# Cross-attention of a decoder layer: the softmax sums of four heads in one group of matmuls

## The chip, the cores and the metric

The kernel runs on one core of a Trainium2 chip. The metric is the time of one execution on the device, in microseconds (us). The engines are PE (matrix multiplication), DVE (vector), ACT (scalar functions), POOL (GpSimd) and SP (here it only issues DMAs). Each works through its own queue of instructions in order; they wait for each other by semaphores.

## What is computed

One decoder layer over 4 x 512 tokens of width 512, in fp32: self-attention (32 heads of 16, causal), cross-attention, and a feed-forward part with quantised weights and activations, each on the layer norm of its input and added to it. The change lies in the cross-attention:

```
qh = q.reshape(b * h, d // h, m)          # b = 4, h = 8: 32 heads of 64 rows
kh = k.reshape(b * h, d // h, -1)         # k and v are both the context
vh = v.reshape(b * h, c // h, -1)
qk = einsum('bdm,bdn->bmn', qh, kh) / sqrt(d // h)
sm = softmax(qk, axis=-1)                 # over 512 columns n
ret = einsum('bmn,bcn->bcm', sm, vh)      # 64 rows x 512 per head
x = x + ret
```

## The kernel before

`rest_of_layer` (line 891) holds three parts: the output projection of self-attention (`attend_output`), the cross-attention (`attend_context`) and the feed-forward part (`feed`). `in_turn` (line 972) gives each engine the same order of steps, so the order in which an engine meets its work is written out by hand: attention steps i = 3 to 43, and from step 36 on a feed body beside each (body 2 beside step 36, and so on); then the rest of the feed bodies, up to body 19.

The 32 heads go in 16 pairs p. Head j of a pair uses half of the partitions. The stages of one pair lie several steps apart; `pair_due(i, behind)` says which pair is due in step i, and gives one in every second step only. In a step i the engines meet:

- PE: two rounds of F (`first_scores`, line 1592: two matmuls, for head i - 1, each into one of three PSUM banks) and S (`second_scores`, line 1612: eight matmuls for head i - 4, with a row of maxima subtracted; banks from a pool of four). Then, in even steps, the sum of pair (i - 8) / 2 (`sum_probs`, line 1651) and half of W (`weigh`, line 1637: probabilities times context) of pair (i - 6) / 2; in odd steps the other half of W, of pair (i - 5) / 2.
- DVE: four reductions (line 1416), each of which frees a bank of F. A fourth F of a step needs the bank that the step's first reduction frees (three banks). In even steps the total of the pair's second head (line 1446) stands between the first two, a reciprocal (line 1453) between the second and third, a subtraction for the keys (line 1428) between the third and fourth, and a transpose of the maxima (line 1422) at the end. In odd steps y is multiplied by the inverse sums (line 1465) at the end.
- POOL: in even steps `halves` of the first head (line 1175, waits for DVE's total of the pair before) and its total (line 1180), in odd steps `halves` of the second head, then the addition of y to the tokens `tok` (line 1184).
- ACT: four exponentials (line 1277), the copy of W's result to y (`keep_weighted`, line 1252), in even steps the copy of the keys and of the sum (`keep_sums`, line 1301, to `den`), in odd steps two small DMAs that spread `den` over 16 partitions (`few`).
- SP: in odd steps the maxima rows (four DMAs, line 1044), context and query rows and the store of the inverse sums to memory (line 1097); in even steps their load, spread over 64 partitions each (`rden`, two DMAs, line 1105).

The sum over the 512 keys is a matmul with ones: two column halves of the array give the sums of the two heads of a pair on 64 partitions each. What is summed is `total`, the four key blocks already added up (first head on POOL, second on DVE). The division is put off until after W: y times `rden`.

Sums 0 to 13 stand in the even steps 8 to 34, sum 14 at the end of step 36, sum 15 in feed body 4. In steps 24 and 27 DVE also takes the moments of the first token tiles (`token_moments`, lines 1384 and 1387), in 33 and 34 it scales them (line 1473 on); POOL has their deviations in 25 and 28 (line 1142) and rounds them in 33 and 34 (line 1190). Step 35 ends with the rounding and turning of the first token tile (ACT lines 1313, 1367), on which feed body 2 begins: gate and up (PE, line 1698), SiLU (ACT, line 1327), product (DVE, line 1500).

Of the kernel before, what the change touches and what calls it, by code (L numbers as in the profile page):

```python
# [13 lines left out]
P = 128  # L14
# [876 lines left out]
def rest_of_layer(nc, io, scr, keep, out):  # L891
# [5 lines left out]
    PAIRS = HEADS_X // 2  # L897
    SCALE = float(XROWS) ** -0.5
    BANKS = 3
    PSLOTS, QSLOTS, LSLOTS = 5, 4, 3  # L900
    NB = FF // 512
    with ExitStack() as ctx:
# [18 lines left out]
        halves = m.sb("halves", [P, 2, DIM]); total = m.sb("total", [P, UNROLL, DIM])  # L921
        mx = m.sb("mx", [P, 2, H // 2]); mt = m.sb("mt", [P, 2, H // 2])
        den = m.sb("den", [P, DIM]); few = m.sb("few", [2 * RUNS, 2, H]); inv = m.sb("inv", [2 * RUNS, 2, H])
        rden = m.sb("rden", [P, DIM]); y = m.sb("y", [P, UNROLL, DIM])
# [34 lines left out]
        few_in, inv_done, inv_out, rden_in = (m.sem(s) for s in ("few_in", "inv_done", "inv_out", "rden_in"))  # L959
# [6 lines left out]
        C_LAST, D_LAST, E_LAST = TILES + 3, HEADS_X + 12, TILES + 4  # L966
# [29 lines left out]
        for i in range(1, D_LAST):  # L996
            for n in range(STEP):
                if 0 <= i - 1 < HEADS_X:
                    p1_use["f", i, n] = len(p1_use)
            for n in range(STEP):  # L1000
                if 0 <= i - 4 < HEADS_X:
                    p2_use["s", i - 4, n] = len(p2_use)
            if i >= 8 and i % 2 == 0 and (i - 8) // 2 < PAIRS:
                p2_use["sum", (i - 8) // 2] = len(p2_use)
        P1_USES, P2_USES = len(p1_use), p2_use["s", HEADS_X - 1, STEP - 1] + 1
        LATE_SUMS, LAST_SUM_BODY = PAIRS - 2, E_FIRST + 2
# [4 lines left out]
        def p2_bank(*key):  # L1011
            return p2[SBANKS - 1] if key[0] == "sum" and key[1] >= LATE_SUMS else p2[p2_use[key] % SBANKS]

        def pair_due(i, behind):

            s = i - behind
            return s // 2 if s >= 0 and s % 2 == 0 and s < HEADS_X else None

        @block.sync
        def _(sp):  # L1020
# [53 lines left out]
            def attend_context(i):  # L1074
# [19 lines left out]
                p = pair_due(i, 11)  # L1094
                if p is not None:
                    sp.wait_ge(inv_done, p + 1)
                    sp.dma_start(scr["inv"][2 * RUNS * p:2 * RUNS * (p + 1), :], inv[:, p % 2, :]).then_inc(inv_out, 16)
                p = pair_due(i, 12)
                if p is not None:
                    sp.wait_ge(inv_out, 16 * (p + 1))  # L1100
                    if due(p):
                        sp.wait_ge(y_done, p)
                    for a in range(2):
                        at = RUNS * (2 * p + a)
                        sp.dma_start(rden[a * H:(a + 1) * H, :], scr["inv"][at:at + RUNS, :].rearrange("r c -> (r c)")
                                     .unsqueeze(0).broadcast_to([H, DIM])).then_inc(rden_in, 16)
# [22 lines left out]
        def _(pool):  # L1129
# [34 lines left out]
            def attend_context(i):  # L1164
                j = i - 6
                if 0 <= j < HEADS_X:
                    p, a = j // 2, j % 2
                    if a == 0:
                        pool.wait_ge(p2_used, p2_use["s", 2 * p + 1, STEP - 1] + 1)
                        if due(p):  # L1170
                            pool.wait_ge(second_total, p)
                    else:
                        pool.wait_ge(first_total, p + 1)
                    slot = 2 * (p % 2) + a
                    nc.gpsimd.tensor_tensor(halves[:], probs[:, slot, 0:2, :], probs[:, slot, 2:4, :], ALU.add).then_inc(halved, 1)  # L1175
                    if a == 0:
                        pool.wait_ge(halved, j + 1)
                        if due(p - 1):
                            pool.wait_ge(summed, p - 1)
                        nc.gpsimd.tensor_tensor(total[:, slot, :], halves[:, 0, :], halves[:, 1, :], ALU.add).then_inc(first_total, 1)  # L1180
# [42 lines left out]
        def _(act):  # L1223
# [28 lines left out]
            def keep_weighted(p):  # L1252
                act.wait_ge(weighted, p + 1)
                if due(p - UNROLL + 1):
                    act.wait_ge(x2_done, p - UNROLL + 1)
                nc.scalar.activation(y[:, p % UNROLL, :], pn[:], ACT.Copy).then_inc(y_kept, 1)  # L1256

            def attend_context(i):
# [24 lines left out]
                p = pair_due(i, 9)  # L1283
# [561 lines left out]
```

## Time and profile before

| | us |
|---|---|
| median of 3 runs | 789.53 (788.87, 789.53, 791.5) |
| the profiled execution | 791.34 |
| its span in the trace | 789.5 |

| engine | busy us | share of the span |
|---|---|---|
| PE | 758.5 | 96% |
| DVE | 637.8 | 81% |
| ACT | 491.1 | 62% |
| POOL | 423.1 | 54% |

The trace begins and ends inside the execution, so its span is shorter than the execution's own time. TensorE's granted clock was 0.994 of its full speed over the span. All starts below are counted from the start of the span. The self-attention ends at about 371, the cross-attention's steps run to about 600, the feed-forward part to the end. Busy times are not work: an engine that holds an instruction that is blocked inside it counts as busy.

### The profile page before, as it was taken

What the parts mean: (1) busy time and instruction counts of PE and PEld (TensorE: products, weight loads), DVE (VectorE), ACT (ScalarE), POOL (GpSimd) and SP (SyncE); (2) the same over time, 40 slices, a digit from 0 to 9 for tenths busy, and PEclk for the clock granted to TensorE, in tenths of its full rate; (3) what the DMA queues carried; (4) which work ended last, traced back from release to release, by engine and by line L of the source; (5) the groups of instructions that cost most, each with busy time, mean ns of one, the idle gap of its engine ahead of it and who ended that gap; (6) DMA issues with size and microseconds to landing.
All of it is one profiled execution on the core that took longest, in us unless ns stands there. A gap on an engine that the chain in (4) does not pass through costs nothing.

```text
span 789.5 us, 15365 instructions
## 1 busy us (share of the span) xinstructions
PE 758.5 (96%) x4832; PEld 420.6 (53%) x4886; DVE 637.8 (81%) x1905; ACT 491.1 (62%) x844; POOL 423.1 (54%) x459
## 2 busy tenths in 40 slices
PE   8999999999999999998999899999998999999998
PEld 6777544444444444443777555555543455455543
DVE  7676888889888889881589878888977899888883
ACT  4665567667766776676355555555556576567564
POOL 5554489999999700000234367777886444423331
PEclk9999999999999999999899999999999999999999
DMA  8898674444544311200486434444420011000001
GB/s 289 301 385 282 210 186 136 122 132 133 139 128 130 96 54 52 61 18 3 146 284 236 162 108 136 134 136 135 121 70 18 11 42 41 28 15 27 28 26 42
DMA packets 65888, 94.79 MB, mean 120 GB/s; under 512 B 27184, under 2 KB 38576, under 8 KB 64272
## 3 DMA queue, kind: packets, MB, share of 16 engines
q1 hardware_dynamic: 61344, 80.77, 32.5%
q0 software_dynamic: 3952, 12.98, 5.8%
q8 instruction: 39, 0.64, 0.3%
q14 instruction: 41, 0.34, 0.1%
q10 hardware_dynamic: 512, 0.07, 0.1%
HBM read 72.88 MB, written 20.51 MB: 118 GB/s over the span
## 4 chain that ended last, share of the span: by engine, by line
PE 40%; DVE 5%; issue 3%; ACT 2%; POOL 1%; SPq 0%; DMA 0%; ACTq 0%; DVEq 0%; POOLq 0%
PE r_p L1698 12%; PE r_p L1633 7%; PE r_pn L1646 7%; PE r_p L1728 3%; PE r_pn L1728 3%; PE r_p L1605 3%; PE r_p L1661 2%; PE r_p L1712 2%; DVE r_stats L1384 1%; DVE tok L1403 1%; PE r_p L1587 1%; DVE r_xl L1397 1%; ACT r_xn L1235 1%; DVE r_mx L1416 0%; DVE r_h L1500 0%
## 5 line engine op out<-in xcount | busy, mean ns | idle before, releaser
L787 ACT ACTIVATE b_probs<-ab_j 128x512 f32<-128x512 f32 (+1 forms) x352 | 176.7, 560 | 25.5 <-PE ab_j L852 14.6
L148 DVE CUSTOM_DVE_ANT_0 b_junk<-ab_t,mask_qk 128x128 bf16<-128x128 f32 (+2 forms) x243 | 108.7, 485 | 27.0 <-PE ab_t L128 26.7
L852 PE MATMUL ab_j<-qs,ks 98*128 98x512 bf16 (+1 forms) x352 | 121.8, 361 | 2.9 <-DMA qs<-mrow 1.1
L1277 ACT ACTIVATE r_probs<-r_p 128x512 f32<-128x512 f32 x128 | 69.5, 599 | 65.2 <-PE r_p L1633 63.8
L148 DVE CUSTOM_DVE_ANT_0 b_junk<-ab_e,mask_qk 128x256 bf16<-128x256 f32 (+2 forms) x237 | 103.6, 482 | 0.3 <-issue 0.2
L1416 DVE TENSOR_REDUCE r_mx<-r_p 128x1 f32<-128x512 f32 x128 | 82.4, 675 | 22.1 <-PE r_p L1605 21.2
L1175 POOL TENSOR_TENSOR r_halves<-r_probs 128x1024 f32<-128x1024 f32 x32 | 76.6, 2395 | 34.8 <-DVE r_total L1446 24.9
L1327 ACT ACTIVATE r_silu<-r_p,r_cg 128x512 f32<-128x512 f32 x64 | 44.2, 691 | 53.0 <-PE r_p L1698 51.7
L870 PE MATMUL ab_pv<-b_probs,v 128*32 128x512 f32 (+3 forms) x1024 | 75.6, 436 | 0.0
L1202 POOL TENSOR_SCALAR r_h<-r_h,r_fh 128x1024 f32<-128x1024 f32 x32 | 38.0, 1199 | 64.8 <-DVE r_fh L1546 64.8
L128 PE MATMUL ab_e<-ks,qs 96*128 96x128 bf16 (+3 forms) x269 | 64.0, 300 | 5.3 <-DVE mx L148 0.7
L1698 PE MATMUL r_p<-wu,r_zt 128*128 128x512 bf16 x251 | 65.4, 379 | 0.3
L1698 PE MATMUL r_p<-wg,r_zt 128*128 128x512 bf16 x245 | 63.5, 379 | 2.1 <-ACT r_zt L1367 1.4
L1646 PE MATMUL r_pn<-r_probs,r_vt 128*64 128x512 f32 x256 | 61.3, 599 | 0.5 <-ACT r_y L1256 0.5
L128 PE MATMUL ab_t<-ks,qs 96*128 96x128 bf16 (+2 forms) x243 | 58.6, 301 | 2.4 <-DVE mx L148 0.2
L1500 DVE TENSOR_TENSOR r_h<-r_p,r_silu 128x512 f32<-128x512 f32 x64 | 44.0, 687 | 18.7 <-PE r_p L1698 10.7
L870 PEld LDWEIGHTS ab_pv<-b_probs,v 128*32 128x32 f32 x1024 | 30.0, 109 | 48.3 <-issue 41.6
L1130 POOL MEMSET r_mrows<- 128x1024 f32 x1 | 1.0, 952 | 101.7 <-POOLq L238 101.7
L797 ACT ACTIVATE b_osb<-ab_pv 128x512 f32<-128x512 f32 x32 | 19.1, 597 | 58.2 <-PE ab_pv L870 58.2
L852 PEld LDWEIGHTS ab_j<-qs,ks 98*128 98x128 bf16 x352 | 34.1, 97 | 26.5 <-ACT b_probs L787 10.4
L1508 DVE TENSOR_REDUCE r_hpart<-r_h 128x1 f32<-128x512 f32 x64 | 43.9, 686 | 2.2
L128 PEld LDWEIGHTS ab_e<-ks,qs 96*128 96x128 bf16 x269 | 22.9, 98 | 39.6 <-DVE mx L148 14.8
(177 smaller groups left out, 1761.3 us busy)
## 6 DMA issues: line engine op xcount, KB each, us to landing
qs<-q_parts SPq DMA_DIRECT2D x32, 192.0 KB, 3.3
q_parts<-a_parts SPq DMA_DIRECT2D x15, 384.0 KB, 6.1
a_wst<-in_w_gate SPq DMA_DIRECT2D x4, 1024.0 KB, 7.7
a_wst<-in_w_up SPq DMA_DIRECT2D x4, 1024.0 KB, 9.9
a_wst<-in_w_down SPq DMA_DIRECT2D x4, 1024.0 KB, 8.3
qs<-q_parts SPq DMA_DIRECT2D x32, 128.0 KB, 3.2
b_wst<-in_w_gate POOLq DMA_DIRECT2D x16, 256.0 KB, 3.8
b_wst<-in_w_up POOLq DMA_DIRECT2D x16, 256.0 KB, 3.3
```

The lines of the kernel that those rows point to most:

```text
L128: last = nc.tensor.matmul(st.bank(keep, i, k)[:, c:c + w], keep["qs"][0:STACK, s, j, qt * P:(qt + 1) * P], keep["ks"][0:STACK, s, 0:w], st ...
L148: best = nc.vector.tensor_tensor_reduce(out=junk[:, 2 * (st.use[i, k] % slots) + n, 0:w], in0=bank[:, c:c + w], in1=keep["mask_qk"][:, SEQ ...
L787: nc.scalar.activation(pblock(j % 2, kb)[:, j0:j0 + nj, c:c + w], p2[(NE * j + n) % BANKS2][:, 0:nj * w].rearrange("p (j c) -> p j c", j=n ...
L852: last = nc.tensor.matmul(bank, ks[0:STACK + 2, s, kb * P:(kb + 1) * P], qs[0:STACK + 2, s, j0:j0 + nj, kb * P + c:kb * P + c + w], start= ...
L870: last = nc.tensor.matmul(pv[2 * HDIM * j:2 * HDIM * (j + 1), kb * P:], v, pblock(j3 % 2, kb)[:, j, :], start=kb == 0, stop=kb == TPB - 1, ...
L1175: nc.gpsimd.tensor_tensor(halves[:], probs[:, slot, 0:2, :], probs[:, slot, 2:4, :], ALU.add).then_inc(halved, 1)
L1277: nc.scalar.activation(probs[:, 2 * (p % 2) + a, blk, :], p2_bank("s", j, n)[:], ACT.Exp, scale=SCALE).then_inc(p2_used, 1)
L1416: nc.vector.reduce_max(mx[:, p % 2, KD * a + blk:KD * a + blk + 1], p1_bank("f", i, n)[:], AX.X).then_inc(p1_used, 1)
L1633: last = nc.tensor.matmul(p2_bank("s", j, 2 * b + a)[:], weights, right[rows, :], start=term == 0, stop=term == 3)
L1646: last = nc.tensor.matmul(pn[a * H:(a + 1) * H, :], vt[:, 2 * (p % 2) + a, nb, :], probs[:, 2 * (p % 2) + a, nb, :], start=nb == 0, stop=n ...
L1698: last = nc.tensor.matmul(bank[g % len(bank)][:], zt[:, j % 2, k, :], keep[w][:, k, n * 512:(n + 1) * 512], start=k == 0, stop=k == KD - 1)
L1728: last = nc.tensor.matmul(pf[j % 2][:], ht[j % 2][:, k, :], keep["wd"][:, k, :], start=k == 0, stop=k == KF - 1)
```

## The change

- The 32 heads' sums are taken in 8 groups of four (`q`), with 32 columns of ones and 32 partitions of the result for each head, in every fourth step (4q + 10) instead of every second. The last group is summed in feed body 4, where sum 15 was; there is none at the end of step 36.
- Copy, spreading DMA (now one, of 4 partitions), reciprocal, store and load of the inverse sums follow at steps 4q + 10, 11, 12, 13 and 14. Four `rden` loads stand together, into two buffers.
- The scaling of y and the addition to `tok` come for the two pairs of a group in steps 4q + 15 and 4q + 16 (`scaled_pair`), where they came in every odd step. `y` has 5 buffers instead of 4, `total` has 8 instead of 4 and lies where the output weights were; the first one waits for the last projection.
- There is one more attention step (44), with feed body 10 beside it.

```diff
-        C_LAST, D_LAST, E_LAST = TILES + 3, HEADS_X + 12, TILES + 4
+        C_LAST, D_LAST, E_LAST = TILES + 3, HEADS_X + 13, TILES + 4
...
+        def scaled_pair(i):
+
+            s = i - 15
+            return s // 4 * 2 + s % 4 if s >= 0 and s % 4 < 2 and s < HEADS_X else None
+
+        def quad_due(i, behind):
+
+            s = i - behind
+            return s // 4 if s >= 0 and s % 4 == 0 and s < HEADS_X else None
...
+                q = quad_due(i, 13)
+                if q is not None:
+                    sp.wait_ge(inv_done, q + 1)
+                    sp.dma_start(scr["inv"][4 * RUNS * q:4 * RUNS * (q + 1), :], inv[:, q % 2, :]).then_inc(inv_out, 16)
+                q = quad_due(i, 14)
+                if q is not None:
+                    sp.wait_ge(inv_out, 16 * (q + 1))
+                    for p in (2 * q, 2 * q + 1):
+                        if due(p - 1):
+                            sp.wait_ge(y_done, p - 1)
+                        for a in range(2):
+                            at = RUNS * (2 * p + a)
+                            sp.dma_start(rden[a * H:(a + 1) * H, p % 2, :], scr["inv"][at:at + RUNS, :].rearrange("r c -> (r c)")
+                                         .unsqueeze(0).broadcast_to([H, DIM])).then_inc(rden_in[p % 2], 16)
...
-                p = pair_due(i, 13)
+                p = scaled_pair(i)
                 if p is not None:
                     pool.wait_ge(y_done, p + 1)
-                    nc.gpsimd.tensor_tensor(tok[:, p, :], y[:, p % UNROLL, :], tok[:, p, :], ALU.add).then_inc(x2_done, 1)
+                    nc.gpsimd.tensor_tensor(tok[:, p, :], y[:, p % YSLOTS, :], tok[:, p, :], ALU.add).then_inc(x2_done, 1)
...
+                q = quad_due(i, 11)
+                if q is not None:
+                    act.wait_ge(p2_used, p2_use["sum", q] + 1)
+                    if due(q - 1):
+                        act.wait_ge(inv_done, q - 1)
+                    act.dma_start(few[:, q % 2, :], den[0:3 * PART + 1:PART, :].rearrange("a (r c) -> a r c", r=RUNS)).then_inc(few_in, 16)
...
+                q = quad_due(i, 12)
+                if q is not None:
+                    dve.wait_ge(few_in, 16 * (q + 1))
+                    if due(q - 1):
+                        dve.wait_ge(inv_out, 16 * (q - 1))
+                    nc.vector.reciprocal(inv[:, q % 2, :], few[:, q % 2, :]).then_inc(inv_done, 1)
...
-                p = pair_due(i, 13)
+                p = scaled_pair(i)
                 if p is not None:
-                    dve.wait_ge(rden_in, 32 * (p + 1))
+                    dve.wait_ge(rden_in[p % 2], 32 * (p // 2 + 1))
                     dve.wait_ge(y_kept, p + 1)
-                    nc.vector.tensor_tensor(y[:, p % UNROLL, :], y[:, p % UNROLL, :], rden[:], ALU.mult).then_inc(y_done, 1)
+                    nc.vector.tensor_tensor(y[:, p % YSLOTS, :], y[:, p % YSLOTS, :], rden[:, p % 2, :], ALU.mult).then_inc(y_done, 1)
...
-                for a in range(2):
-                    last = nc.tensor.matmul(p2_bank("sum", p)[a * H:(a + 1) * H, :], keep["ones64"][:], total[:, 2 * (p % 2) + a, :], start=True, stop=True)
+                for a in range(4):
+                    last = nc.tensor.matmul(p2_bank("sum", q)[a * PART:(a + 1) * PART, :], keep["ones64"][:, 0:PART], total[:, (4 * q + a) % TSLOTS, :],
+                                            start=True, stop=True)
                 last.then_inc(summed, 1)
...
-                p = pair_due(i, 8)
-                if p is not None and p < LATE_SUMS:
-                    sum_probs(p)
+                q = quad_due(i, 10)
+                if q is not None and q < QUADS - 1:
+                    sum_probs(q)
...
-                if i == 2 * LATE_SUMS + 8:
-                    sum_probs(LATE_SUMS)
```

## Rows read from the trace of the kernel before

**Rows 1.** Windows, one pair of steps: length, busy time (instructions) by engine, clock, DMA.
```profile
487.85:497.72 9.87, 9.87 (x63) 5.35 (x64) 8.33 (x14) 5.73 (x12) 7.67 (x5) 1.00 0.51 143
```

**Rows 2.** Timeline, PE, steps 16 and 17: start, us, engine, line, operation, tiles, count.
```profile
495.02 0.50 PE L1605 MATMUL r_p<-r_kh,r_qh 64*128 64x512 f32 x2
...
497.21 0.51 PE L1633 MATMUL r_p<-r_mrows,r_unit 64*128 64x512 f32 x2
497.65 1.08 PE L1661 MATMUL r_p<-r_total,ones 128*64 128x512 f32 x4
...
500.38 0.49 PE L1605 MATMUL r_p<-r_kh,r_qh 64*128 64x512 f32 x2
...
501.64 0.51 PE L1605 MATMUL r_p<-r_kh,r_qh 64*128 64x512 f32 x2
...
504.87 0.50 PE L1605 MATMUL r_p<-r_kh,r_qh 64*128 64x512 f32 x2
```

**Rows 3.** Timeline, DVE, same steps; in brackets the idle time before and its releaser.
```profile
498.36 1.53 DVE L1428 TENSOR_TENSOR r_kl<-r_k,r_kh 128x512 fp32r<-128x512 f32 x1
...
500.54 0.21 DVE L1422 STREAM_TRANSPOSE r_mt<-r_mx 128x32 f32<-128x32 f32 x1
...
500.91 2.48 DVE L1416 TENSOR_REDUCE r_mx<-r_p 128x1 f32<-128x512 f32 x4 [0.16 <-PE r_p L1605]
...
503.31 0.75 DVE L1465 TENSOR_TENSOR r_y<-r_y,r_rden 128x512 f32<-128x512 f32 x1
```

**Rows 4.** Timeline, POOL, same steps.
```profile
496.98 2.37 POOL L1175 TENSOR_TENSOR r_halves<-r_probs 128x1024 f32<-128x1024 f32 x1 [1.42 <-DVE r_total L1446]
...
499.43 1.61 POOL L1180 TENSOR_TENSOR r_total<-r_halves 128x512 f32<-128x512 f32 x1
...
501.11 2.40 POOL L1175 TENSOR_TENSOR r_halves<-r_probs 128x1024 f32<-128x1024 f32 x1
...
504.14 1.28 POOL L1184 TENSOR_TENSOR tok<-r_y,tok 128x512 f32<-128x512 f32 x1 [0.63 <-DVE r_y L1465]
```

**Rows 5.** Timeline, PE and DVE, steps 24 and 25, with moments on DVE.
```profile
534.37 0.50 PE L1605 MATMUL r_p<-r_kh,r_qh 64*128 64x512 f32 x2
...
540.04 0.65 DVE L1384 BATCH_NORM_STATS2 r_stats<-tok 128x6 f32<-128x512 f32 x1
...
540.94 2.45 DVE L1416 TENSOR_REDUCE r_mx<-r_p 128x1 f32<-128x512 f32 x4
...
541.65 0.49 PE L1605 MATMUL r_p<-r_kh,r_qh 64*128 64x512 f32 x1 [0.29 <-DVE r_mx L1416]
```

**Rows 6.** Timeline, PE, self-attention: product in four quarters, and what follows it.
```profile
252.71 2.36 PE L870 MATMUL ab_pv<-b_probs,v 128*32 128x512 f32 x32
255.01 0.39 PE L128 MATMUL ab_t<-ks,qs 96*128 96x128 bf16 x2
```

**Rows 7.** Timeline, end of step 35 to the first product of feed body 2.
```profile
591.61 1.57 ACT L1277 ACTIVATE r_probs<-r_p 128x512 f32<-128x512 f32 x3 [0.50 <-issue]
...
595.65 2.35 POOL L1175 TENSOR_TENSOR r_halves<-r_probs 128x1024 f32<-128x1024 f32 x1 [0.69 <-DVE r_total L1446]
595.85 1.03 PE L1661 MATMUL r_p<-r_total,ones 128*64 128x512 f32 x4
...
597.04 0.81 PE L1698 MATMUL r_p<-wg,r_zt 128*128 128x512 bf16 x3 [0.16 <-issue]
597.54 1.28 ACT L1327 ACT_TABLE_LOAD   x1
...
599.56 0.69 DVE L1500 TENSOR_TENSOR r_h<-r_p,r_silu 128x512 f32<-128x512 f32 x1 [3.60 <-ACT r_silu L1327]
```

**Rows 8.** Timeline, DMA issues on SP, steps 16 and 17.
```profile
498.79 1.15 SPq L1105 DMA_DIRECT2D r_rden<-inverse_sums  x2
...
500.77 2.22 SPq L1044 DMA_DIRECT2D r_mrows<-r_mt  x4
```

**Rows 9.** Windows, ten us of the feed bodies.
```profile
696.00:706.00 10.00, 9.95 (x62) 5.12 (x61) 8.98 (x22) 5.89 (x10) 3.25 (x4) 1.00 0.07 27
```

More of the change, by code:

```diff
@@ L920, in rest_of_layer @@
         vt = m.sb("vt", [P, UNROLL, KD, H])
-        halves = m.sb("halves", [P, 2, DIM]); total = m.sb("total", [P, UNROLL, DIM])
+        halves = m.sb("halves", [P, 2, DIM]); total = over("total", [P, TSLOTS, DIM], nc.sbuf_top)
         mx = m.sb("mx", [P, 2, H // 2]); mt = m.sb("mt", [P, 2, H // 2])
-        den = m.sb("den", [P, DIM]); few = m.sb("few", [2 * RUNS, 2, H]); inv = m.sb("inv", [2 * RUNS, 2, H])
-        rden = m.sb("rden", [P, DIM]); y = m.sb("y", [P, UNROLL, DIM])
+        den = m.sb("den", [P, DIM]); few = m.sb("few", [4 * RUNS, 2, H]); inv = m.sb("inv", [4 * RUNS, 2, H])
+        rden = m.sb("rden", [P, 2, DIM]); y = m.sb("y", [P, YSLOTS, DIM])
         stats = m.sb("stats", [P, 2, 6]); mv = m.sb("mv", [P, 2, 2]); rstd = m.sb("rstd", [P, 2]); shift = m.sb("shift", [P, 2]); veps = m.sb("veps", [P, 2])
@@ L1011, in p2_bank @@
         def p2_bank(*key):
-            return p2[SBANKS - 1] if key[0] == "sum" and key[1] >= LATE_SUMS else p2[p2_use[key] % SBANKS]
+            return p2[SBANKS - 1] if key == ("sum", QUADS - 1) else p2[p2_use[key] % SBANKS]
         def pair_due(i, behind):
@@ L1296, in attend_context, with keep_sums @@
                 exponential(3)
-                p = pair_due(i, 8)
-                if p is not None and p < PAIRS - 1:
-                    keep_sums(p)
-            def keep_sums(p):
-                act.wait_ge(summed, p + 1)
-                if due(p):
-                    act.wait_ge(few_in, 32 * p)
-                nc.scalar.activation(den[:], p2_bank("sum", p)[:], ACT.Copy).then_inc(p2_used, 1)
+                q = quad_due(i, 10)
+                if q is not None and q < QUADS - 1:
+                    keep_sums(q)
+            def keep_sums(q):
+                act.wait_ge(summed, q + 1)
+                if due(q):
+                    act.wait_ge(few_in, 16 * q)
+                nc.scalar.activation(den[:], p2_bank("sum", q)[:], ACT.Copy).then_inc(p2_used, 1)
             def quantised(j):
@@ L1667, in attend_context @@
                     second_scores(i - 4, b)
-                p = pair_due(i, 8)
-                if p is not None and p < LATE_SUMS:
-                    sum_probs(p)
+                q = quad_due(i, 10)
+                if q is not None and q < QUADS - 1:
+                    sum_probs(q)
                 p = pair_due(i, 5)
@@ L1721, in down @@
                         elif j == 1:
-                            pe.wait_ge(p2_used, p2_use["sum", PAIRS - 1] + 1)
+                            pe.wait_ge(p2_used, p2_use["sum", QUADS - 1] + 1)
                         else:
```

81 lines of the change are left out of this document (27 added, 54 removed).

## The prediction

> Times are microseconds. I write t for the start of an even attention step (its first F) and give what follows relative to it; the sample step is i = 16, t = 495.02.
>
> **What bounds the kernel now.** I read the page first: PE is busy 96% of the span (in the table of the times), which says only that PE is nearly always holding something. The windows of one pair of heads (two steps) say more: in 9.87, PE is busy throughout, DVE 8.33, POOL 7.67, ACT 5.73 [rows 1]. So DVE has 1.5 to spare per pair on average, and a shorter PE seems to pay in full. The timeline shows that it doesn't, and the reader should put three lists side by side.
> PE [rows 2]: the even step runs 495.02 to 500.38 = 5.36 with its sum, the odd one 500.38 to 504.87 = 4.49 without. So a sum costs 0.87. The second F of the odd step starts at 501.64, t + 6.62.
> DVE [rows 3]: its reductions feed the three F banks. The fourth F block of a step needs the bank that the same step's first reduction frees. That reduction starts at 500.91 after waiting 0.16 for PE; DVE was free at 500.54 + 0.21 = 500.75, t + 5.73. So at the end of an even step DVE is a mere 0.16 ahead.
> POOL [rows 4]: the subtraction of L1428 starts at 498.36 and ends at 499.89, which is 0.54 after POOL's halves end (496.98 + 2.37 = 499.35). A DVE operation on two SBUF tensors waited for the POOL operation. The halves start when DVE's total of the same step ends, so this chain (maximum, total, halves, subtraction, maximum, transpose) is as long as before however soon PE is ready; dropping the reciprocal before it doesn't shorten it.
> A case of DVE being later stands in the trace: step 24 adds a moments pair on DVE after the transpose. The reduction starts at 540.94, the F that waits for it at 541.65, 0.71 later and with 0.29 of idle PE put down to DVE; t was 534.37, so that F is at t + 7.28 instead of 6.62 [rows 5].
>
> **The change, part by part.**
> The sums. Sixteen sums of two heads become eight of four. Does the second pair ride along free? The nearest row is the self-attention's product over 32 columns each, four heads side by side, fp32 with 128 rows: 16 matmuls, 1280 columns per head, 252.71 to 255.01 = 2.30 [rows 6]. At that price per column four heads of 512 columns take 512 / 1280 x 2.30 = 0.92, hardly more than two heads take now (0.87). Seven such sums stay in even steps 10, 14, .. 34, the eighth in feed body 4. Steps 8, 12, .. 32 lose theirs. I add 0.1 to each remaining sum for 0.92 against 0.87 and for one more change of array shape: + 0.7 (0 to + 1.4). The upper end is from the gap before a sum: the last score block starts at 497.21 + 0.23 + 0.23 = 497.44 to 497.65 away, so a change costs at most some 0.2 [rows 2].
> The Trainium skill, TensorEngine Tiling (Array Packing), Key Properties, says that changing the tiling mode drains the TensorE, which speaks against a lone 32-column group between 64-column ones. By that rule the seven sums would pay the 1.4 end; where tiles merely run beside each other they pay nothing.
> Steps 8 and 12 (no sum, nothing added on DVE). PE could be at its fourth F 0.87 earlier, but that F waits for DVE, which is free 0.16 earlier than it was used. Gain 0.16 each: - 0.3.
> Steps 16, 20, 28 (no sum, and more on DVE). The scaling of y now comes in steps 4q + 15 and 4q + 16. Before, all of it lay in odd steps, where DVE idles. Half of it now lands behind the transpose of just those even steps that lost their sum. DVE is free at 5.73; POOL's total runs until 499.43 + 1.61 = t + 6.02, and the scaling reads two SBUF tensors, so it ends 0.54 after that, 6.56; by its own 0.75 it would end at 6.48 [rows 3, 4]. The reduction follows and the F 0.71 after it: 7.27, less an overlap of up to 0.1 between neighbouring DVE rows, against 6.62. So + 0.6 each (0.4 to 0.65): + 1.8. All work behind this F on PE (S, W, the next step) shifts with it.
> The Trainium skill, SBUF — State Buffer, section SBUF: two separate sides, calls this shared port pair an exclusive lock held for the whole instruction, against VectorE operations with two SBUF inputs. By it the scaling ends at 6.56, without it at 6.48; the row of L1428 agrees (0.54 behind POOL).
> Step 24 has both the scaling and the moments: 0.83 of scaling goes on top of 7.28: + 0.8.
> Step 32: the last F is in this step, so no F waits for DVE in 33. The 0.87 of the sum may come back in full, or be eaten by the maxima row that S of step 34 waits for, whose chain is the same as before. I take - 0.4 (0 to - 0.87).
> The transition (steps 35 and 36, feed body 2). One few-DMA instead of two in step 35: ACT's three exponentials waited 0.50 on issue for it: - 0.45. The sum of step 36 leaves: from 595.85 to the gate's 597.04, 1.1. The copy of that sum leaves ACT, so that the table load (1.28 from 597.54) happens while ACT idles and the first SiLU waits for its gate only: - 0.7 more. Together - 2.3. But DVE now has a scaling of y (pair 11) before the first product, and POOL's halves of step 36 stand at 595.65 to 598.00, released by DVE's total of that step; the scaling ends 0.54 behind them, 598.54. I let this POOL work come 0.5 earlier, since DVE and POOL have less to do in steps 33 to 35: the first product starts at 598.1 instead of 599.56, - 1.45 (- 0.9 to - 2.3) [rows 7].
> At nothing: the eight reciprocals, eight copies of sums and 24 few-DMAs that go lie in ACT's and DVE's idle time (ACT 5.73 of 9.87); their cover is not needed again. SP's order: the four rden DMAs of an even step stand in front of the maxima DMAs of the next odd step. Two of them took 1.15 from t + 3.77; four would end at t + 6.07, 0.32 after the maxima DMAs began before (500.77, t + 5.75) [rows 8]. Those would then be issued by t + 8.3 and are wanted by the S of the next step, over 1.5 later; I cost it at nothing, 0.3 a quad if that cover is thin. The wait for y_done in front of them names a scaling two steps past. POOL's addition to tok (1.28) moves with the scaling, between its total and its second halves: 6.56 + 1.28 + 2.40 puts the end of these at about t + 10.3, and DVE's total, which asks for them, starts over 1.0 into the next even step, at t + 11.5 [rows 4]: covered by about 1.0. The extra attention step and later scalings beside feed bodies 5, 6, 9 and 10 are hidden: there PE is busy 9.95 of 10 and DVE 8.98 [rows 9]. Totals over the output weights cost nothing in time: the wait for the last projection is long past.
> The sum: - 0.3 + 0.7 + 1.8 + 0.8 - 0.4 - 1.45 = + 1.15. The profiled execution took 791.34 with a span of 789.5, so 1.84 lie around the span; the median of the three runs, 789.53, is 1.8 below the profiled one. A difference made of the span carries over to the median: 789.53 + 1.15 = 790.7.
>
> **The rivals.**
> A, PE is what counts: if DVE's order has more give than the 0.16, seven steps give 0.87 and the transition 2.3, less the 0.7: - 7.7, 781.8. For it speaks DVE's average of 8.33 in 9.87; against it the F of step 24, which was late by just what DVE was late.
> B, the scaling finds a gap (it runs ahead of POOL's total, or F tolerates it): six steps at - 0.16, + 0.7, - 0.4, - 1.45 = - 2.1, 787.4. Against it: the operation stands in DVE's order before the reduction that PE needs.
> C, slower: POOL becomes late. With the addition to tok in front of its second halves, the DVE total of the next even step must wait, then the halves, the subtraction and the F follow late. It decides from a lateness of 1.0, and steps 25 and 28, with the deviations on POOL as well, are nearest to it. Price: about 0.5 in each of four pairs, and the transition gains nothing, as POOL's halves bound it there: + 1.15 + 2.0 + 1.45, 794.1.
> D, four quarters don't run beside each other but two after two: eight sums at 0.87 more, 790.7 + 7.0 = 797.7. The 32-column row speaks against it: four heads side by side took 0.92 per 512 columns there.
>
> **How the numbers follow.** Forecast 0.55, A 0.10, B 0.12, C 0.20, D 0.03. A measurement tells about 0.3% (2.4) from no change. Faster is A, half of B and a small tail of the forecast, whose terms reach - 1.6 at their best: 0.18. Slower is most of C, D and a tail, whose terms reach + 3: 0.27. The rest, 0.55, is within. The range leaves out A and D and keeps most of B and C: 786.5 to 794.5.
>
> **What would show it.** Right: pairs of steps with a quad sum stay at 9.9 to 10.0; steps 16, 20, 28 have pairs of 10.3 to 10.5 with an F of PE idle until DVE's L1416, and the y scaling directly before it; step 24's pair is near 11.3; steps 8 and 12 near 9.7; a quad sum takes 0.9 to 1.0 to the next W; the first product comes 1.5 earlier after the last W. Wrong: pairs without sum at 9.0 (A), no idle PE before that F (B), halves of POOL or a DVE total waiting in steps 18, 22, 26 (C), a quad sum of 1.8 (D). The sum is wrong if the feed bodies from the fifth on change length.

## The result, and the profile after

The changed kernel takes 791.84 us (median of 20 executions, 789.64 to 794.44) against 789.73 of the kernel before on the same chip (20 executions, 788.4 to 791.61): ratio 1.0025, 95% interval 1.0015 to 1.0035. It is 2.1 us slower; the interval leaves out 1, but the difference is only about a quarter of a per cent. The profiled execution took 794.38 with a span of 792.6, so its span is 3.1 longer than the one of before, which is more than the 2.1 of the medians. It is not a typical execution: its mean granted clock over the span is 0.989, and of the 20 executions only three have 0.988 or 0.989 (794.28, 794.38 and 794.44); the other 17 have 0.994 to 0.998 and take 789.64 to 793.47.

The page after, busy time of the engines:

```profile
PE 757.0 (96%) x4832; PEld 418.1 (53%) x4886; DVE 636.0 (80%) x1897; ACT 486.5 (61%) x836; POOL 423.7 (53%) x459
```

PE, DVE and ACT are busy for 1.5, 1.8 and 4.6 us less than before, and the kernel is not faster: the sum of busy time says nothing here. The windows of four pairs of steps do; the columns are those of [rows 1]:

```profile
455.96:465.53 9.57, 9.36 (x59) 4.92 (x58) 7.54 (x11) 5.24 (x10) 6.39 (x3) 1.00 0.30 82
485.12:495.11 9.99, 9.99 (x67) 5.21 (x66) 8.35 (x12) 5.62 (x11) 7.07 (x4) 1.00 0.53 162
495.11:505.58 10.47, 9.40 (x58) 4.92 (x58) 8.42 (x13) 5.24 (x10) 8.19 (x5) 1.00 0.44 131
536.06:549.07 13.01, 11.01 (x58) 5.20 (x58) 9.19 (x15) 5.35 (x10) 8.79 (x7) 0.87 0.52 153
```

They are the pairs of steps 8, 14, 16 and 24. In the pair with a sum (the second line) PE is busy throughout. In the pairs without one PE is busy for only 9.36 to 9.40, less than the 9.87 of [rows 1], and yet the third pair is 10.47 long: 1.07 of it is idle PE. The sums left PE, and idle time took their place.

The timeline of steps 16 and 17 after, POOL, DVE and PE together, to be put beside [rows 2 to 4] (t = 495.04, against 495.02 before):

```profile
497.01 2.37 POOL L1188 TENSOR_TENSOR r_halves<-r_probs 128x1024 f32<-128x1024 f32 x1 [1.30 <-DVE r_total L1457]
498.39 1.54 DVE L1439 TENSOR_TENSOR r_kl<-r_k,r_kh 128x512 fp32r<-128x512 f32 x1
499.46 1.63 POOL L1193 TENSOR_TENSOR r_total<-r_halves 128x512 f32<-128x512 f32 x1
...
500.56 0.21 DVE L1433 STREAM_TRANSPOSE r_mt<-r_mx 128x32 f32<-128x32 f32 x1
500.70 0.93 DVE L1476 TENSOR_TENSOR r_y<-r_y,r_rden 128x512 f32<-128x512 f32 x1
501.56 1.87 DVE L1427 TENSOR_REDUCE r_mx<-r_p 128x1 f32<-128x512 f32 x3
502.29 0.50 PE L1616 MATMUL r_p<-r_kh,r_qh 64*128 64x512 f32 x1 [1.07 <-DVE r_mx L1427]
```

The transpose is where it was (500.54 before). Behind it stands the scaling of y; it takes 0.93 and ends at 501.63, 0.54 after POOL's total (499.46 + 1.63 = 501.09). Then comes the reduction, and the F that waited for it starts at t + 7.25, where it started at t + 6.62.

Step 24, to be put beside [rows 5]:

```profile
541.66 0.93 DVE L1476 TENSOR_TENSOR r_y<-r_y,r_rden 128x512 f32<-128x512 f32 x1
542.51 0.68 DVE L1395 BATCH_NORM_STATS2 r_stats<-tok 128x6 f32<-128x512 f32 x1
...
543.43 2.45 DVE L1427 TENSOR_REDUCE r_mx<-r_p 128x1 f32<-128x512 f32 x4
544.14 0.50 PE L1616 MATMUL r_p<-r_kh,r_qh 64*128 64x512 f32 x1 [2.00 <-DVE r_mx L1427]
545.60 3.47 PE L1657 MATMUL r_pn<-r_probs,r_vt 128*64 128x512 f32 x8
549.00 0.50 PE L1616 MATMUL r_p<-r_kh,r_qh 64*128 64x512 f32 x2
```

Here the scaling and the moments stand one behind the other, and PE idles for 2.00. Behind that idle time half of W takes 3.47, where it takes 1.94 elsewhere. The windows of those microseconds tell why:

```profile
545.00:547.00 2.00, 2.00 (x9) 0.67 (x7) 0.88 (x2) 1.09 (x2) 1.83 (x3) 0.58 0.84 273
547.00:549.00 2.00, 2.00 (x6) 0.24 (x2) 0.00 (x0) 0.00 (x0) 0.22 (x1) 0.57 0.98 253
```

The granted clock is 0.58 and 0.57 of full speed on average, so for most of the time it was at the lower of its two levels, 1.2 GHz.

The transition to the feed-forward part, against [rows 7]:

```profile
586.12 1.52 POOL L1197 TENSOR_TENSOR tok<-r_y,tok 128x512 f32<-128x512 f32 x1 [0.62 <-DVE r_y L1476]
587.60 2.38 POOL L1188 TENSOR_TENSOR r_halves<-r_probs 128x1024 f32<-128x1024 f32 x1
590.02 0.69 DVE L1457 TENSOR_TENSOR r_total<-r_halves 128x512 f32<-128x512 f32 x1 [2.17 <-POOL r_halves L1188]
590.81 1.07 PE L1670 MATMUL r_p<-r_total,ones 128*32 128x512 f32 x8 [0.49 <-DVE r_total L1457]
...
600.44 0.81 PE L1706 MATMUL r_p<-wg,r_zt 128*128 128x512 bf16 x3 [0.16 <-issue]
600.50 3.07 POOL L1188 TENSOR_TENSOR r_halves<-r_probs 128x1024 f32<-128x1024 f32 x1 [0.69 <-DVE r_total L1457]
600.75 0.62 DVE L1476 TENSOR_TENSOR r_y<-r_y,r_rden 128x512 f32<-128x512 f32 x1
602.23 0.69 DVE L1511 TENSOR_TENSOR r_h<-r_p,r_silu 128x512 f32<-128x512 f32 x1 [0.86 <-PE r_p L1706]
```

With the starts of F, this gives the ledger of the two spans. Forecast is the term of the prediction's sum. The second turn is the one in which PE turns h of feed body 2 for the second time (612.17 before, 615.25 after).

| stretch | before | after | difference | forecast |
|---|---|---|---|---|
| start to F of step 6 | 446.60 | 446.89 | + 0.29 | 0 |
| pairs 8, 12 | 9.84, 9.85 | 9.57, 9.60 | - 0.52 | - 0.3 |
| pairs 10, 14, 18, 22, 26, 30 (a sum each), and the sum's shape in step 34 | 9.83 to 9.87 | 9.98 to 10.00 | + 0.86, + 0.13 | + 0.7 |
| pairs 16, 20, 28 | 9.83 to 9.86 | 10.47, 10.47, 10.48 | + 1.87 | + 1.8 |
| pair 24, up to its late F | 7.28 | 8.15 | + 0.87 | + 0.8 |
| pair 24, behind it | 3.21 | 4.86 | + 1.65 | 0 |
| steps 32, 33 | 9.59 | 8.76 | - 0.83 | - 0.4 |
| the rest of step 34 | | | + 0.56 | 0 |
| step 35 to the first product | 10.76 | 8.55 | - 2.21 | |
| first product to the second turn | 12.61 | 13.02 | + 0.41 | |
| these two together | | | - 1.80 | - 1.45 |
| the rest, to the end | 177.33 | 177.35 | + 0.02 | 0 |
| sum | | | + 3.1 | + 1.15 |

Without the 1.65 behind the late F of pair 24 the span would have grown by 1.45.

### The profile page after: what moved, and what is told of

It reads as the page before. It is cut to its first block, busy times and chain, and to the rows that moved or that the text cites. A ratio compares the mean times of both kernels' runs of the same rounds, so it can differ in the third digit from the quotient of the medians.

```text
span 792.6 us, 15273 instructions
## 1 busy us (share of the span) xinstructions
PE 757.0 (96%) x4832; PEld 418.1 (53%) x4886; DVE 636.0 (80%) x1897; ACT 486.5 (61%) x836; POOL 423.7 (53%) x459
## 4 chain that ended last, share of the span: by engine, by line
PE 36%; DVE 10%; issue 3%; ACT 2%; POOL 2%; DVEq 0%; POOLq 0%; ACTq 0%
PE r_p L1706 12%; PE r_pn L1657 6%; PE r_p L1644 5%; PE r_p L1736 3%; PE r_pn L1736 3%; PE r_p L1616 3%; DVE r_mx L1427 2%; PE r_p L1720 2%; DVE r_kl L1439 1%; DVE r_stats L1395 1%; PE r_p L1670 1%; DVE tok L1414 1%; PE r_p L1598 1%; DVE r_xl L1408 1%; DVE r_y L1476 1%
## 5 line engine op out<-in xcount | busy, mean ns | idle before, releaser
L1657 PE MATMUL r_pn<-r_probs,r_vt 128*64 128x512 f32 x256 | 63.5, 618 | 0.5 <-ACT r_y L1269 0.5
L1511 DVE TENSOR_TENSOR r_h<-r_p,r_silu 128x512 f32<-128x512 f32 x64 | 44.1, 690 | 16.3 <-PE r_p L1706 10.7
L1616 PE MATMUL r_p<-r_kh,r_qh 64*128 64x512 f32 x128 | 36.9, 484 | 7.8 <-DVE r_mx L1427 7.8
```

Of the source, the lines that this page charges most:

```text
L1616: nc.tensor.matmul(p1_bank("f", i, n)[:], qh[rows, p % QSLOTS, blk * P:(blk + 1) * P], kh[rows, p % UNROLL, :], start=True, stop=True).the ...
L1657: last = nc.tensor.matmul(pn[a * H:(a + 1) * H, :], vt[:, 2 * (p % 2) + a, nb, :], probs[:, 2 * (p % 2) + a, nb, :], start=nb == 0, stop=n ...
```

## The experiments

Two theories had to be told apart. The forecast's: each F that is late waits for DVE, and DVE is late because of what stands in its queue behind the transpose of an even step (the scaling, the moments) and before it (the subtraction for the keys, which waits for POOL's halves). Its rivals: the PE work itself grew (four quarters not side by side, or the change of shape), or POOL became late.

**e1: the scaling moved off the even steps** (the loop over the scalings ends one step later for it).

```
             s = i - 15
-            return s // 4 * 2 + s % 4 if s >= 0 and s % 4 < 2 and s < HEADS_X else None
+            return s // 2 if s >= 0 and s % 2 == 0 and s < HEADS_X else None
```

> The changed kernel with both scalings of a group in odd steps (4q + 15 and 4q + 17 instead of 4q + 15 and 4q + 16), one attention step more. Theory (the scaling behind the transpose of an even step makes DVE late for the F that PE runs next): pairs from steps 16, 20, 28 fall from 10.47 to the 9.58 of steps 8 and 12, that of step 24 from 13.0 to about 10.3, and the sum of step 34 no longer waits for DVE's total (0.5): 4.5 to 6 us less than the changed kernel, 786 to 787.5. Rival (the place of the scaling doesn't matter, four-head sums themselves or the DMA order cost the time): unchanged, 791.8.

Measured: 788.42 (12 executions, 785.49 to 789.16), ratio to before 0.9971 (0.9958 to 0.9983), so 4.3 us less than the changed kernel by the two ratios. That is a little less than the 4.5 to 6 expected, and 0.9 above the upper end of the range for the time. The timeline shows the reduction directly behind the transpose and 0.19 of idle PE in place of 1.07:

```profile
497.59 0.21 DVE L1433 STREAM_TRANSPOSE r_mt<-r_mx 128x32 f32<-128x32 f32 x1
497.73 2.44 DVE L1427 TENSOR_REDUCE r_mx<-r_p 128x1 f32<-128x512 f32 x4
498.43 0.50 PE L1616 MATMUL r_p<-r_kh,r_qh 64*128 64x512 f32 x1 [0.19 <-DVE r_mx L1427]
```

The odd steps 17, 21 and 29 fell from 5.97 to 5.10, step 25 from 8.51 to 5.98. The scaling in the wrong step is thus a cause, and its price is as in the sum. Yet odd steps still take 5.1 and not the 4.5 that their PE work takes: something before the transpose holds DVE as well.

**e2: the subtraction for the keys moved to the odd steps.**

```
                 maximum(i, 2)
-                p = pair_due(i, 2)
+                maximum(i, 3)
+                p = pair_due(i, 1)
                 if p is not None and p >= 1:
                     keys_low(p)
-                maximum(i, 3)
+                p = pair_due(i, 2)
```

> The changed kernel with one move: the subtraction for the low part of the keys on DVE goes from the even step 2p + 2, where it stands behind POOL's halves, to the end of the odd step 2p + 1. Theory (the chain total, halves on POOL, subtraction, maximum, transpose sets when DVE is ready): the even steps' chain ends some 1 us earlier even with the scaling, so that all pairs without a sum take 9.0 and keep PE busy: steps 8 and 12 save 0.6 each, 16, 20, 28 1.5 each, 24 between 1.6 and 3.3, about 8 in all: 783 to 785. Rival (PE isn't held by that chain, or the subtraction collides with POOL's second halves in the odd step and delays the next even step as much): no gain, 791 to 792.

Measured: 785.92 (6 executions, 783.16 to 787.96), ratio 0.9945 (0.9925 to 0.9965). Steps 9, 13, 17, 21 and 29 are 4.48 to 4.51 long: no F waits for DVE there any more, although the scaling still stands in front of the reduction of step 17. The median is 0.9 above the expected range, and the timeline shows where the rest went: steps 18 and 22 grew to 6.05 and step 30 to 5.60.

```profile
496.98 1.28 POOL L1197 TENSOR_TENSOR tok<-r_y,tok 128x512 f32<-128x512 f32 x1
498.22 2.36 POOL L1188 TENSOR_TENSOR r_halves<-r_probs 128x1024 f32<-128x1024 f32 x1
...
498.40 2.74 DVE L1439 TENSOR_TENSOR r_kl<-r_k,r_kh 128x512 fp32r<-128x512 f32 x1
501.06 0.68 DVE L1427 TENSOR_REDUCE r_mx<-r_p 128x1 f32<-128x512 f32 x1
501.79 0.50 PE L1617 MATMUL r_p<-r_kh,r_qh 64*128 64x512 f32 x1 [0.18 <-DVE r_mx L1427]
```

The subtraction met the second halves of POOL, which the addition to tok had delayed, and again ended 0.56 behind them (501.14 against 500.58). It had been moved from one POOL operation to the next.

**e6: both together**, the two edits above in one kernel:

> Both moves together on the changed kernel: scalings in steps 4q + 15 and 4q + 17, the keys' subtraction in odd steps. With the subtraction alone, steps 18 and 22 still took 6.05 instead of 5.49: in the odd step before them the subtraction ended 2.74 after its start, behind POOL's addition to tok and its halves. Theory (that is POOL's lateness, brought by the addition in the even step): with the scaling in odd steps all sum steps take 5.49 and all others 4.50, some 1.2 less than with the subtraction alone, about 784.5. Rival (the two DVE operations in one odd step are too much and delay the next even step): pairs over 9.1 or 10.1 and 786 or more.

Measured: 785.23 (6 executions, 783.61 to 787.7), ratio 0.9948 (0.993 to 0.9967). Steps with a sum take 5.49, the others 4.50, but for step 28 (5.06) and step 30 (5.95). So without DVE in the way the pairs take 9.99 with a sum and 9.00 without one, as long as their PE work. The 1.2 less than e2 that were expected do not show in the time: the ratio is that of e2 (0.9945), on another chip. In the profiled executions the stretch from the F of step 6 to the first product is shorter by 0.84 (146.15 against 146.99), but the one before it is longer; why is found at e5.

**e3: the moments of the first token tile one step earlier.**

```
             def first_tokens(i):
-                if i == 24:
+                if i == 23:
                     token_moments(0)
```

> The changed kernel with the moments of the first token tile in step 23 instead of 24 on DVE. Theory: the F of step 25 waits only for the scaling then; PE's idle stretch there falls from 2.0 to about 1.3, the pair loses 0.87 of stall, and the granted clock doesn't fall behind it (it was 0.58 for about 3 us, which cost 1.65): pair of step 24 at 10.5 instead of 13.0, 790 to 791 in the median, and a narrower spread of the runs than 789.6 to 794.4. Rival (the clock falls for another reason): the pair stays over 12, the spread stays.

Measured: 789.28 (12 executions, 788.19 to 792.11), ratio 0.9993 (0.9979 to 1.0008): 2.5 us less than the changed kernel by the ratios, and 0.7 below the expected range.

```profile
539.85 0.50 PE L1616 MATMUL r_p<-r_kh,r_qh 64*128 64x512 f32 x1 [1.07 <-DVE r_mx L1427]
541.19 1.94 PE L1657 MATMUL r_pn<-r_probs,r_vt 128*64 128x512 f32 x8
```

Step 25 fell from 8.51 to 5.93, by 2.58. The DVE time taken out of PE's way accounts for 0.93 of that (idle PE 1.07 against 2.00), the clock, which did not fall here (W takes 1.94), for the other 1.65. That is one profiled execution of each kernel. The executions spread over 3.9 us (12) against 4.8 (20), so the narrower spread that was expected is not clearly there. With the edits of e1 and e2 and this one (e8):

> As the last one, and the moments of the first token tile in step 23 too. Theory: step 25 falls to 4.5 as well and PE has no idle stretch left between steps 5 and 32, 0.5 to 0.7 less than the last one: about 784. Rival: three DVE operations at the end of step 23 make DVE late for step 24, and the gain is lost there.

Measured: 785.54 (6 executions, 784.04 to 786.93), ratio 0.9952 (0.9937 to 0.9968). The 0.5 to 0.7 that were expected do not come: step 25 was already at 4.49 in e6.

**e4: the kernel before with DVE made late.** Does the lateness of DVE lengthen a step in the kernel before as well? One more reduction of 512 columns, whose result nobody reads, stands behind the transpose of each even step.

```
                     turn_maxima(p)
+                    nc.vector.reduce_max(spare[:, 0:1], keep["wu"][:, 0, 0:512], AX.X)
...
```

> The kernel before with one extra DVE reduction of about 0.6 (512 bf16 elements of a weight tile into a spare column) behind the transpose of the even steps 4 to 32; its result isn't used. It measures what DVE time in this place costs with every sum still there. Theory (0.16 of slack): 0.4 to 0.45 for each of about 14 pairs, 6 us more than before, 795 to 797. Rival (DVE has 1.5 of idle time in a pair and the banks decouple it): same as before, 789.7.

Measured: 794.78 (6 executions, 793.63 to 796.2), ratio 1.0063 (1.0046 to 1.0081), + 5.0, just under the 795 to 797 expected.

```profile
500.27 0.21 DVE L1422 STREAM_TRANSPOSE r_mt<-r_mx 128x32 f32<-128x32 f32 x1
500.41 0.64 DVE L1461 TENSOR_REDUCE r_spare<-wu 128x1 f32<-128x512 bf16 x1
500.97 2.47 DVE L1416 TENSOR_REDUCE r_mx<-r_p 128x1 f32<-128x512 f32 x4
```

Odd steps went from 4.50 to 4.83, step 25 from 5.15 to 5.73. The operation takes 0.56 from start to start (500.41 to 500.97); where DVE had been ahead 0.34 of it shows, and where it had already been late (25) all of it, 0.58. So DVE's lead at that place was 0.2, not the 1.5 that its busy share suggests. Rival A is refuted for the kernel before.

**e5 and e12: the keys in the kernel before.** If that lead is so small, moving the subtraction there as well should gain what was lost in step 25, and no more. e5 is the edit of e2 in the kernel before.

> The kernel before with the keys' subtraction in odd steps. It tells whether that move is worth something by itself or only makes room for the sums' gain. Theory: PE sets the pace of the kernel before (9.86 a pair with DVE 0.16 ahead), so only the 0.66 of step 25 comes back: 789.1, no change that shows. Rival (the chain over POOL already costs the kernel before something in each pair): pairs under 9.8, 787 or less.

Measured: 792.15 (10 executions, 790.24 to 793.14), ratio 1.0026 (1.0013 to 1.0039): slower, not what was expected. The steps did what they should (sum 5.36, odd 4.50, step 25 4.49), apart from step 28 (5.67). The loss that the profiled execution shows is ahead of them: from the last matmul of the projection to the F of step 6 it took 15.1, against 13.4 before. Those 1.7 are not all of the 2.5 between the medians; the rest is not traced.

```profile
436.97 0.68 DVE L1428 TENSOR_TENSOR r_kl<-r_k,r_kh 128x512 fp32r<-128x512 f32 x1
437.57 1.28 DVE L1397 TENSOR_TENSOR r_xl<-r_xn,r_xh 128x512 fp32r<-128x512 f32 x2
```

The first pair's subtraction now stands in step 3, before the last subtractions of the layer norm. Counted from the first F of step 3 (432.51 here, 433.51 before), the reductions behind them start at 6.27 instead of 5.65, an F of the next step waits 0.20 for DVE, and the granted clock stays low for longer (0.50 from 440 to 444, against 0.68 before). All four kernels with this move take 14.0 to 15.1 for the stretch (e2, e5, e6, e8), the nine others 13.1 to 13.8. So in e12 only the pairs from p = 2 on were moved:

```
                 p = pair_due(i, 2)
-                if p is not None and p >= 1:
+                if p == 1:
                     keys_low(p)
...
                     turn_maxima(p)
+                p = pair_due(i, 1)
+                if p is not None and p >= 2:
+                    keys_low(p)
```

> The kernel before with the keys' subtraction in odd steps, from pair 2 on only. With pair 1 too it was 2.5 slower than before although its steps 6 to 32 took 0.4 less. Theory: the loss is the seam (pair 1's subtraction in step 3), so this one is at 789.0 to 789.5, and not slower than before. Rival (the loss lies elsewhere, in what the new order does to the clock at the output projection or to the feed bodies): it stays at 791 to 792.

Measured: 789.08 (11 executions, 788.26 to 791.71) against 790.96 of the kernel before on that chip, ratio 0.9989 (0.9976 to 1.0003). Leaving that one subtraction in place took the loss away, and the stretch is back at 13.6. So the place of e5's loss is shown. Its mechanism is not: how much of it is DVE's lateness and how much the longer low clock, and whether the one brought the other, no run separates. That the matmuls of the queries waited for the later subtractions, as the expectation of e11 has it, no row shows. The time itself lies in the expected range partly because this chip is slower: the kernel before takes 790.96 on it, not 789.7.

**e11: the change with all of this**: both scalings in odd steps, the subtraction moved from p = 2 on as in e12, and POOL's second deviation one step later.

```
-                elif i == 28:
+                elif i == 29:
                     deviation(S, 1)
```

> The changed kernel with the scalings in odd steps and the keys' subtraction in odd steps from pair 2 on; that of pair 1 stays in step 4. On POOL the deviation of the second token tile moves from step 28 to 29. Theory: the three kernels that moved the subtraction of pair 1 into step 3 put it in front of the last two subtractions of the output projection, on which the seam to the attention steps waits; the stretch from the last projection matmul to step 6 was 14.4 and 14.6 with both moves against 13.1 with the scalings' alone, part of it at half the clock. So 1.2 less than there; and steps 28 and 30, at 5.1 and 5.95, fall to 4.5 and 5.49, another 1.0: 783 to 783.8 in the median. Rival (the seam's length is the clock's chance and not the subtraction; step 30 is late by other POOL work): 785.2 as before these two edits.

Measured: 784.37 (6 executions, 781.42 to 785.84) against 790.96, ratio 0.9913 (0.9892 to 0.9933): 6.9 us less than before by the ratio, and the fastest of all these kernels. (The expected 783 to 783.8 is meant for a chip on which the kernel before takes 789.7; by the ratio that would be 782.9.) In the profiled execution 145.73 lie between the F of step 6 (446.50) and the first product (592.23), against 152.96 before and 155.34 in the changed kernel. What the sums of four heads are worth with DVE's order put right is best read from e11 against e12, on the same chip: 784.37 against 789.08 (POOL's deviation is moved in e11 alone).

```profile
548.83 1.28 DVE L1439 TENSOR_TENSOR r_kl<-r_k,r_kh 128x512 fp32r<-128x512 f32 x1
550.04 0.68 DVE L1479 TENSOR_TENSOR r_y<-r_y,r_rden 128x512 f32<-128x512 f32 x1
550.64 0.68 DVE L1395 BATCH_NORM_STATS2 r_stats<-tok 128x6 f32<-128x512 f32 x1
...
551.56 0.66 DVE L1427 TENSOR_REDUCE r_mx<-r_p 128x1 f32<-128x512 f32 x1
...
552.28 0.49 PE L1619 MATMUL r_p<-r_kh,r_qh 64*128 64x512 f32 x1 [0.23 <-DVE r_mx L1427]
```

The later deviation brought step 30 back to 5.49. Step 28 remained at 5.08 where 4.5 was expected: at the end of step 27 the subtraction, the scaling and the second tile's moments stand in a row on DVE, so a little of what rival A counted on is still missing.

**The price of the quad sum.** Two kernels take the sum's matmuls apart. e9 leaves out two of the four quarters, e10 takes two halves of 64 columns instead, as the kernel before did; both leave out the sums of two heads in four.

```
-                for a in range(4):
+                for a in range(2):
                     last = nc.tensor.matmul(p2_bank("sum", q)[a * PART:(a + 1) * PART, :], ...
```

> The changed kernel with two of the four column quarters in each sum; the sums of the other two heads are left out. A quad sum took 0.99 against 0.86 for the pair sums before. Theory (four quarters run side by side and the 0.13 is the price of the shape): steps with a sum stay at 5.45 to 5.49. Rival (each quarter more costs something): 5.42 or less, in proportion to the matmuls left out. Total time unchanged within 1.

Measured, one execution each: 794.57 (the profiled execution of the changed kernel took 794.38), span 792.8; steps with a sum 5.48, against 5.49 with all four quarters. Leaving out half of the matmuls saves 0.01. And with halves:

```
-                    last = nc.tensor.matmul(p2_bank("sum", q)[a * PART:(a + 1) * PART, :], keep["ones64"][:, 0:PART], ...
+                    last = nc.tensor.matmul(p2_bank("sum", q)[a * H:(a + 1) * H, :], keep["ones64"][:], ...
```

> The changed kernel with sums in the shape of before (64 columns, two heads) at the changed kernel's places; the sums of the other two heads are left out. With two quarters instead of four the steps with a sum took 5.48, as with four. Theory (the 0.13 is the price of one more change of the array's shape): the steps with a sum fall to 5.36. Rival (it is the price of eight buffers, of the later place or of the position behind S): they stay at 5.48.

Measured: 793.3, span 791.5; steps with a sum 5.35, as before. The rows are from step 14 of e10 and, below them, from step 18 of the changed kernel:

```profile
489.18 1.08 PE L1670 MATMUL r_p<-r_total,ones 128*64 128x512 f32 x4
490.09 1.89 PE L1657 MATMUL r_pn<-r_probs,r_vt 128*64 128x512 f32 x8
```

```profile
508.14 1.07 PE L1670 MATMUL r_p<-r_total,ones 128*32 128x512 f32 x8
509.14 1.94 PE L1657 MATMUL r_pn<-r_probs,r_vt 128*64 128x512 f32 x8
```

From the sum's start to W's it is 0.91 with halves and 1.00 with quarters. The rest is in W: 1.89 behind a sum in its own shape (128*64), 1.94 behind the quarters (128*32), and 1.94 too where W follows S (64*128). So the quarters bring a second change of shape, one behind the sum as well as one before it. The second pair of heads rides along free; what costs is the shape, 0.13 to 0.14 a sum step. This kernel gave something else: the same late F in pair 24, behind 1.98 of idle PE, and no fall of the clock.

```profile
545.15 0.50 PE L1616 MATMUL r_p<-r_kh,r_qh 64*128 64x512 f32 x1 [1.98 <-DVE r_mx L1427]
...
546.51 1.94 PE L1657 MATMUL r_pn<-r_probs,r_vt 128*64 128x512 f32 x8
```

Its step 25 is 6.87 long, so pair 24 is 6.87 + 4.50 = 11.4. In e9 the same F also waited for 1.98, and there the clock fell (0.68 and 0.50 in the same two windows):

```profile
545.86 3.55 PE L1657 MATMUL r_pn<-r_probs,r_vt 128*64 128x512 f32 x8
```

Of three profiled executions with this gap two had the fall; of the ten without it none had a fall at that place.

## Why the prediction was right, and where its steps were off

The time (790.7 forecast, 791.84 measured; + 1.15 against + 2.1), the range and the likeliest class (within 0.3%) hold. What carried it is the reading of three queues side by side instead of PE's busy share. That the number came so near is in part luck. In the ledger some stretches came out longer than forecast, by 2.95 together (the clock 1.65, step 34 0.56, the start 0.29, the sums 0.29, small ones 0.16), and others shorter, by 1.00 (steps 32 and 33 0.43, the transition 0.35, steps 8 and 12 0.22), so a third of the misses cancelled.

- **Steps 8 and 12: - 0.52 for - 0.3.** Right in mechanism: DVE was ahead by little, and of a sum of 0.87 only 0.26 a pair came back. I took the lead from DVE's idle 0.16 [rows 3]; e4 measures about 0.2 for it. The rest of the 0.26 is not traced.
- **The sums: + 0.99 for + 0.7.** The shape costs 0.13 to 0.14 each, within its bounds (0 to 0.2), nearer the upper one than I chose. (The working of that upper bound has one 0.23 too many in it: 497.21 + 0.23 = 497.44, and from there to 497.65 it is 0.21; the bound stands.) The quarters do run side by side (D is out: 5.48 and 5.49). The Trainium skill, TensorEngine Tiling (Array Packing), Key Properties, says that a change of mode drains the TensorE. That quarters between halves cost more than halves between halves agrees with it in sign, and so does the place of the cost, on both sides of a change; no run here separates a drain from another cost of the shape.
- **Steps 16, 20, 28: + 1.87 for + 1.8.** Right in place, size and mechanism. The scaling ended 0.54 behind POOL's total, as worked out. e1 took it away and gave back 0.88 in each, more than 0.6, because in e1 these steps also get the gain of a dropped sum, as steps 9 and 13 do. e2 gives all of it back and the missing part of the dropped sum with it: 9.00 a pair.
- **Step 24: + 2.52 for + 0.8, the failed step.** The F came 0.87 later, as forecast. The sum stopped there. It gave PE an idle time of 2 us and didn't ask what the granted clock would do behind it; in the profiled execution the clock fell, and the matmuls at the lower level cost 1.65 more. e3 is the check: without the moments in front, 2.58 went. How many of the 20 executions had this fall is not known (e10 had the gap without it).
- **Steps 32 and 33: - 0.83 for - 0.4.** The whole sum came back. The maxima row did not eat it; the middle of two ends was the wrong choice where no row spoke for the costly one.
- **Step 34: + 0.56 for nothing.** Rival C's mechanism, at one place. In the rows of the transition above the addition to tok, which itself waited 0.62 for the scaling, delays the end of POOL's halves to 589.98, DVE's total waits for them for 2.17, and the quad sum of step 34 for 0.49. In the steps before, the cover of about 1.0 that I worked out held: steps 10 to 30 with a sum are all 5.48 to 5.50. The difference is the time that POOL has: steps 16 and 17 last 10.47 together, steps 32 and 33 only 8.76.
- **The transition: - 1.80 for - 1.45.** The gains are the forecast's upper end (- 2.3), nearly reached (- 2.21), and its parts came as counted: the gate starts 1.48 sooner after the start of step 35 (- 0.45 and - 1.1 were forecast), the first product 0.73 sooner after the gate (- 0.7). But 0.41 of these 0.73 is lost again in the next stretch: from the first gate on, PE's gate and up matmuls run at the same pace as before (6.69 to the next turn of tokens in both kernels), so a sooner first product counts only in part. The sub-step that failed: I let POOL's halves hold the scaling of pair 11. It was the other way round: the scaling ran in 0.62 and the halves took 3.07 instead of 2.35. What came last was PE [0.86 before L1511].
- **The feed bodies: + 0.02**, as forecast.

Without the fall of the clock the terms come to + 1.45. The medians differ by 2.1, the two profiled spans by 3.1; a fall in a part of the executions would lie between. That is an inference: every execution has its mean clock on record, but only profiled ones show where the clock fell, and one of each kernel is profiled.

**Rival A** stood on the right price but on the wrong condition. A kernel in which PE sets nearly all steps exists (e11, ratio 0.9913; rival A's 781.8 would be 0.9902), but only once three pieces of DVE and POOL work are moved; that was no edit of this change. The keys' move alone gives the kernel before 0.9989 (0.9976 to 1.0003), the change alone 1.0025, and together with the odd scalings and POOL's later deviation 0.9913. The change makes PE shorter in steps in which DVE was just in time, so it pays only with DVE's order put right.

## What to carry to other kernels

Before work is taken off a busy engine, look how far the engine that feeds it is ahead at that place, not on average: here 0.2 us, with 1.5 to spare in the pair. Grouping work into fewer, larger pieces bunches its consumers too; write down for each of them which step it lands in, and put it into the steps in which the larger piece runs or the feeding engine idles. And when a stall is costed, cost what it may do to TensorE's clock as well.

## What was not expected of the hardware

- The granted clock behind an idle time of PE of 1.98 to 2.00 us fell to 0.50 to 0.68 in two executions and stayed at 1.00 in a third, with the same instructions around it but for the sum. Behind the idle times of about 1.07 (pairs 16, 20 and 28 of the changed kernel, step 25 of e3) it did not fall.
- Of a DVE and a POOL operation that meet on SBUF tensors either can be the one that is held. DVE's ends lay 0.54 and 0.56 behind POOL's (scaling, subtraction); with the scaling of pair 11 POOL's halves took 3.07 instead of 2.35 and DVE's operation 0.62, although the record of the halves starts 0.25 before that of the scaling (600.50, 600.75). The Trainium skill, SBUF — State Buffer, section SBUF: two separate sides, calls the pair an exclusive lock, and both cases agree with it: 3.07 - 2.35 = 0.72 is about one scaling (0.62).
- Two profiled executions can differ by 2 to 3 us at a place far from the change. At 376 to 380, where the projection part begins, the granted clock was 0.50 in the profiled executions of the kernels before and after and of e9 and e11, 0.56 and 0.57 in e10 and e5, and 1.00 in those of e1, e2, e3, e4, e6, e8 and e12; with 1.00 the projection ended 2.0 to 3.1 us sooner than in the kernel before. That it also makes part of the spread between executions of one kernel is likely, but each kernel has one profiled execution. So spans of single executions are compared here only by stretches that start at the F of step 6. The rows of the kernel before and of e1:

```profile
376.00:380.00 4.00, 3.86 (x9) 3.09 (x10) 0.77 (x2) 0.21 (x1) 0.00 (x0) 0.50 0.58 197
```

```profile
376.00:380.00 4.00, 3.99 (x19) 3.31 (x20) 1.41 (x3) 0.45 (x1) 0.00 (x0) 1.00 0.53 195
```
